# Decoder layer on one core: the feed-forward's preparation stands one batch later in the attention, Pool splits the router's weights, and the last two tiles' statistics go to the feed-forward

## What is computed

```python
x = x + retention(layernorm(x))                       # 8 heads, causal decay
x = x + cross_attention(layernorm(x), ctx, positions) # 32 heads of 16
h = layernorm(x)
router = h @ gate_w.T                                 # 8 experts, softmax, the two best
y = sum of the two chosen experts(h), each weighted by its probability
y = y + sigmoid(h @ shared_gate_w.T) * (silu(h @ s1.T) * (h @ s2.T)) @ sp.T   # 1408 wide
x = x + y
```

## Time and profile before

| | |
|---|---|
| median of 3 runs | 1491.64 us (1490.64 to 1492.25) |
| the profiled execution, its own time | 1494.26 us |
| its span in the profile | 1492.5 us |
| PE busy | 1339.0 us (90%) |
| DVE, ACT, POOL busy | 857.5, 485.4, 510.1 us |
| attention, rounds -1 to 9 | about 396 to 791 us of the span |
| round 7 | about 709 to 757 us |
| rounds 8 and 9 | about 757 to 791 us |
| feed-forward | 791.4 us to the end |

### The profile page before, as it was taken

The page is one execution under the profiler, slowest core; times in us unless marked ns, Lnnn a source line. Parts: engine busy times, 40 slices in busy tenths (PEclk is TensorE's granted clock), DMA queues, the critical chain, the costliest instruction groups (busy, mean ns, idle before and its releaser), DMA issues. The chain is left out here.

```text
span 1492.5 us, 24158 instructions
## 1 busy us (share of the span) xinstructions
PE 1339.0 (90%) x8442; PEld 1074.6 (72%) x8442; DVE 857.5 (57%) x1532; ACT 485.4 (33%) x755; POOL 510.1 (34%) x352
## 2 busy tenths in 40 slices
PE   5899999995499999999878999999999899999980
PEld 4677777773467766767547788888878799999970
DVE  5666666665487878778843556555575522222243
ACT  3222222223256555655645211111111123322320
POOL 1122221224444433335401007541160463575045
PEclk9999999998689999999989999999999999999995
DMA  8970000010565444555400003230000334343247
GB/s 320 324 237 1 0 0 0 0 53 4 182 175 169 139 146 146 157 155 158 122 2 22 1 22 143 90 138 22 22 22 29 134 132 142 134 145 135 82 134 246
DMA packets 84603, 159.83 MB, mean 107 GB/s; under 512 B 8528, under 2 KB 61904, under 8 KB 80976
## 3 DMA queue, kind: packets, MB, share of 16 engines
q1 hardware_dynamic: 78256, 124.19, 26.3%
q0 software_dynamic: 6272, 34.61, 6.6%
HBM read 109.22 MB, written 69.47 MB: 120 GB/s over the span
## 5 line engine op out<-in xcount | busy, mean ns | idle before, releaser
L1684 DVE SCALAR_TENSOR_TENSOR residual<-c_yp,c_shared,residual 128x512 f32<-128x512 f32 x176 | 127.2, 745 | 139.8 <-PE c_yp L43 135.5
L1051 DVE TENSOR_REDUCE b_mx<-b_rt 128x4 f32<-128x1024 f32 x128 | 156.3, 1221 | 54.2 <-PE b_rt L875 54.0
L1210 ACT ACTIVATE b_pf<-b_rt,b_zero 128x1024 f32<-128x1024 f32 x128 | 142.9, 1116 | 131.5 <-PE b_rt L887 131.2
L41 PE MATMUL c_fc<-c_xh,c_w 128*128 128x512 f32 x352 | 137.7, 391 | 0.0
L43 PE MATMUL c_fc<-c_xh,c_w 128*128 128x512 f32 x352 | 137.1, 389 | 0.0
L42 PE MATMUL c_fc<-c_xl,c_w 128*128 128x512 f32 x352 | 137.0, 389 | 0.0
L41 PE MATMUL c_fc<-c_ring,c_xTl 128*128 x312 | 105.2, 337 | 0.0
L1785 ACT ACTIVATE c_s<-c_fc 128x512 f32<-128x512 f32 x44 | 26.3, 598 | 229.3 <-PE c_fc L43 218.2
L43 PE MATMUL c_fc<-c_ring,c_xTh 128*128 x312 | 100.5, 322 | 0.0
L42 PE MATMUL c_fc<-c_ring,c_xTh 128*128 x312 | 100.2, 321 | 0.0
L1698 DVE TENSOR_TENSOR c_hTl<-c_eh,c_hTh 128x384 fp32r<-128x384 f32 x39 | 21.8, 558 | 136.5 <-ACT c_hTh L1809 136.5
(11 more groups left out here) (307 smaller groups left out, 3447.4 us busy)
## 6 DMA issues: line engine op xcount, KB each, us to landing
weights_b<-b_pack SPq DMA_DIRECT2D x128, 200.0 KB
c_eraw<-in_c_we POOLq DMA_DIRECT2D x8, 2176.0 KB, 9.8
b_pack<-b_hi SPq DMA_DIRECT2D x64, 256.0 KB, 2.5
c_rows_in<-in_b_ctx SPq DMA_DIRECT2D x39, 256.0 KB
c_rows_out<-in_b_ctx SPq DMA_DIRECT2D x39, 256.0 KB
c_xe<-c_rows_in SPq DMA_DIRECT2D x39, 256.0 KB, 2.9
c_rows_out<-c_ye SPq DMA_DIRECT2D x39, 256.0 KB, 2.0
c_wraw<-in_c_ws SPq DMA_DIRECT2D x11, 768.0 KB, 4.3
```

The source lines that it names most:

```text
L41: nc.tensor.matmul(out, ll, rh, start=start, stop=False)
L1051: nc.vector.tensor_reduce(out=mx[:, :, 2 * p:2 * p + 2].rearrange("p t e -> p e t"), in_=rt[:, 0:2, :].rearrange("p e (t s) -> p e t s", s ...
L1210: nc.scalar.activation(pf[:, s:s + 2, :], rt[:, 2:4, :], ACT.Exp, scale=XD ** -0.5, bias=zero[:, :]).then_inc(e_done, 1)
L1684: nc.vector.scalar_tensor_tensor(out=X[:, t, :], in0=yp[:, (n * 4 + k) % 3, :], scalar=shared[:, t:t + 1], in1=X[:, t, :], op0=ALU.mult, o ...
```

## The change

Of the lead-in, all but the loads and the last part moves from round 7 to round 8. In detail:

- `lead_shift` and `lead_low` (DVE), `lead_normal` and `lead_high` (ACT) and `lead_turn` (PE) stand in round 8; `lead_normal` at 1 to 4 where it stood at 2 to 5, the others at the same positions as before. `lead_loads` stays in round 7. `lead_turn` waits for one more batch's use of its two banks.
- ACT rounds the router's weights at position 0 of round 8. Pool does the subtraction for their low part, between its two weight splits, all three in one piece at position 0 of round 8, behind a wait for batch 7's last `negate`.
- The statistics of batch 7 (tiles 14, 15) are gone from round 9, and the root on Pool too. They stand at the head of the feed-forward's DVE list, behind `shift_by` of tiles 4 to 13; Pool's root comes after one more constant; `shift_by` of tiles 14, 15 stands behind the first `router_logits`, and ACT waits for it before the last two tiles.

```diff
@@ PE, cross attention
-                        pe.wait_ge(gm_read[BANK["w", n]], uses(B - 3, "w", n))
+                        pe.wait_ge(gm_read[BANK["w", n]], uses(B - 2, "w", n))
-                    if isinstance(b, int) and b == B - 1 and 4 <= i < 8:
+                    if isinstance(b, int) and b == B and 4 <= i < 8:
                         lead_turn(i - 4)
-                    if isinstance(b, int) and b == B - 1 and i == 10:
+                    if isinstance(b, int) and b == B and i == 10:
                         pe.wait_ge(lead.xl_done, 4)
@@ DVE, cross attention
-                    if isinstance(b, int) and b == B - 1:
+                    if isinstance(b, int) and b == B:
                         if i == 0:
                             lead_shift()
                         if 6 <= i < 10:
                             lead_low(i - 6)
-                        if i == 12:
-                            dve.wait_ge(lead.gwh_done, 1)
-                            nc.vector.tensor_tensor(lead.gwl[:, :, :], lead.graw[:, :, :], as_f32(lead.gwh[:, :, :]), ALU.subtract)\
-                                .then_inc(lead.gwl_done, 1)
-                    for d in due(i, live, 36):
-                        final_first(b + d, own)
-                    for d in due(i, live, 37):
-                        final_statistics(b + d, own)
+                    if not (isinstance(b, int) and b > B):
+                        for d in due(i, live, 36):
+                            final_first(b + d, own)
+                        for d in due(i, live, 37):
+                            final_statistics(b + d, own)
@@ ACT, cross attention
-                    if isinstance(b, int) and b == B - 1:
-                        if 2 <= i < 6:
-                            lead_normal(i - 2)
+                    if isinstance(b, int) and b == B:
+                        if 1 <= i < 5:
+                            lead_normal(i - 1)
                         if 5 <= i < 9:
                             lead_high(i - 5)
-                        if i == 11:
+                        if i == 0:
                             act.wait_ge(lead.const_in, 48)
                             nc.scalar.copy(lead.gwh[:, :, :], lead.graw[:, :, :]).then_inc(lead.gwh_done, 1)
@@ Pool, cross attention
-                    if isinstance(b, int) and b == B - 1 and i in (2, 10):
-                        lead_split(i // 10)
+                    if isinstance(b, int) and b == B and i == 0:
+                        pool.wait_ge(nm_done, 4 * B)
+                        lead_split(0)
+                        pool.wait_ge(lead.gwh_done, 1)
+                        nc.gpsimd.tensor_tensor(lead.gwl[:, :, :], lead.graw[:, :, :], as_f32(lead.gwh[:, :, :]), ALU.subtract)\
+                            .then_inc(lead.gwl_done, 1)
+                        lead_split(1)
-                    for d in due(i, live, 38):
-                        final_root(b + d)
+                    if not (isinstance(b, int) and b > B):
+                        for d in due(i, live, 38):
+                            final_root(b + d)
@@ Pool, feed-forward
+            nc.gpsimd.memset(power[:, :], -0.5).then_inc(presets, 1)
+            pool.wait_ge(presets, 4)
             pool.sem_inc(d_done, 1)
+            pool.wait_ge(var_done, 1)
+            nc.gpsimd.tensor_tensor(rstd[:, NT - TB:NT], var[:, NT - TB:NT], power[:, :].to_broadcast([P, TB]), ALU.pow).then_inc(rstd_done, 1)
             split(2)
@@ DVE, feed-forward
-            nc.vector.scalar_tensor_tensor(out=shift_by[:, 4:NT], in0=mean[:, 4:NT], scalar=-1.0, in1=rstd[:, 4:NT],
-                                           op0=ALU.mult, op1=ALU.mult).then_inc(shift_done, 1)
+            def shifts(a, b):
+                nc.vector.scalar_tensor_tensor(out=shift_by[:, a:b], in0=mean[:, a:b], scalar=-1.0, in1=rstd[:, a:b],
+                                               op0=ALU.mult, op1=ALU.mult).then_inc(shift_done, 1)
+
+            shifts(4, NT - TB)
+            for t in range(TB):
+                last = nc.vector.bn_stats(out=st[:, t, :], in_=X[:, NT - TB + t, :])
+            own.step(last)
+            for t in range(TB):
+                last = nc.vector.bn_aggr(out=mv[:, t, :], in_=st[:, t, :])
+            own.step(last)
+            own.step(nc.vector.tensor_copy(mean[:, NT - TB:NT], mv[:, :, 0]))
+            nc.vector.tensor_scalar(var[:, NT - TB:NT], mv[:, :, 1], EPS, None, ALU.add).then_inc(var_done, 1)
             low_x(4, 8)
@@ DVE, feed-forward, behind router_logits(n)
+                if n == 0:
+                    dve.wait_ge(rstd_done, 1)
+                    shifts(NT - TB, NT)
@@ ACT, feed-forward
             def normalize(a, b):
+                if b == NT:
+                    act.wait_ge(shift_done, 3)
```

## The result

| | before | after |
|---|---|---|
| median of 4 runs each | 1491.95 us | 1479.88 us (1477.01 to 1482.22) |
| ratio after to before | | 0.9917, 95% interval 0.9894 to 0.9939 |
| profiled execution, own time | 1494.26 us | 1482.22 us |
| its span | 1492.5 us | 1480.4 us |

Forecast were 1479.6 us and a span of 1480.5. In a second comparison on another occasion (`e8_after_again`, 6 runs beside 17 of before) the ratio was 0.9929, interval 0.9906 to 0.9952. So the change gains some 11 to 12 us. The total is as forecast; the rows behind it are not in every part, and that is what the rest is about.

The account below looks back on a forecast made before the run. PE was taken to bound the kernel, so gains before the feed-forward should arrive whole. Terms 7.3 - 0.7 + 3.0 + 2.4 = 12.0 us took the span from 1492.5 to 1480.5, giving 1479.6 us, range 1476 to 1486.

Parts of the forecast that it names:

- Round 7, (a), positions 5 to 11: Round 7, without the lead-in's transposes: position 12's rows start at 740.0, 2.6 us saved (1.0 to 3.6).
- (b), position 12: Round 7, position 12: taking the router's subtraction out of DVE's list saves 3.5 us (3.1 to 3.9).
- (c), the clock behind it: Round 7, behind PE's 4.93 us wait: products no longer run at the lower clock, 1.2 us saved (0 to 1.2).
- Round 7 in sum: Round 7, its three savings together: 7.3 us, from 4.1 to 8.7.
- Round 8: Round 8, with the lead-in's work added: net cost 0.7 us, between a gain of 1.0 and a cost of 5.6.
- the step on the clock: Round 8, values at position 9: added transposes bring PE to the upper clock level, some 0.9 us less.
- Round 9: Round 9 and the barrier: without the last statistics and Pool's root, PE starts at 788.6 instead of 791.59, 3.0 us saved.
- The clock at `router(0)`: Feed-forward's first products: upper clock from the start after the shorter gap, 2.4 us saved (0 to 2.7).
- The sum: Whole kernel: 7.3 - 0.7 + 3.0 + 2.4 = 12.0 us saved, span 1480.5.
- The signs of being wrong: 723.00 (PE's wait for maxima at round 7's position 4) moves; DVE stretched in round 8; feed-forward off 700.9 beyond 2.4.
- Pool would hold DVE in round 8: Rival, round 8: Pool's long instructions block DVE at the last scaling, up to 3.46 us, 1483.1; chance 0.05.
- The clock did not stay down: Rival: PE, thinly used, stays at the lower clock from 723 until the feed-forward, 16.3 us lost, 1495.9; chance 0.03.

Follow-up runs that it names:

- e8_after_again: The changed kernel itself, without a further edit, measured again on another occasion against the kernel before: ratio 0.9929.
- e9_split_late: The kernel before with only Pool's second weight split moved behind batch 7's last negation in round 8, DVE's subtraction left at position 12: ratio to before 0.9965.
- e2_stats_alone: The kernel before with only the last two tiles' statistics moved from round 9 to the feed-forward: ratio to before 0.9965.
- e3_gwl_alone: The kernel before with only the subtraction for the router's low part moved from DVE in round 7 to Pool in round 8: ratio to before 0.9963.
- e4_split_apart: The kernel before with only Pool's second weight split written at position 14 of round 7 instead of 10; Pool ran it as before: ratio to before 1.0003.
- e10_normal_early: The changed kernel with the shift and ACT's four normalizations back in round 7, transposes and splits still in round 8: ratio to before 0.9935.
- e7_splits_back: The changed kernel with Pool's two weight splits back in round 7, the router's subtraction still on Pool in round 8: ratio to before 0.9931.
- e6_fill: The changed kernel with the last statistics back in round 9, plus 14 useless PE products while they run: ratio to before 0.9931.
- e5_loads_at_2: The changed kernel with only the lead-in's five loads moved from position 1 to position 2 of round 7: ratio to before 0.9914.

## Why the prediction was right, point by point

- **Round 7, (a), positions 5 to 11.** The time of `rows` of position 12 was forecast as 740.0, that is 28.2 behind the first maximum (711.8); it is 744.00, 28.4 behind 715.60. That the total was met is luck, for the parts were not. Forecast were 1.0 up to `rows` of position 5 and 1.6 from there on. Measured are 2.4 up to there (727.03 is 11.43 behind the first maximum, where it was 13.83) and nothing from there on (16.97 to position 12, where it was 16.98). In `e8_after_again` it is 0.7 and 1.8. Over the kernels that mean the same as for the sum below, `rows` of position 12 comes 1.7 sooner. The transfer, too, did not land at a fixed time: it landed 3.0 later, while round 7 began 3.8 later. In the eleven executions with the loads ahead of it PE goes on 10.2 to 11.8 behind the round's first maximum, so it comes with the round.
- **(b), position 12.** Forecast 3.5 (3.1 to 3.9), measured 7.14 to 3.64: 3.5, but for the two executions with the lower clock at position 11 (5.09 and 5.41). The mechanism, DVE held by Pool's instruction, was argued from two rows and is shown by `e9_split_late`.
- **(c), the clock behind it.** Forecast 1.2; the changed kernel's last three positions took 7.42 and in its second execution 6.09, against 7.76, 7.87 and 7.79 of the old order: 0.3 to 1.8. Right in kind, not a number that one execution can give.
- **Round 7 in sum** was forecast as 7.3. Over three executions of the old order (43.56, 42.18, 41.89, mean 42.5) and four of the new one with its loads in place (37.31, 35.91, 38.14, 35.36, mean 36.7) it is 5.9. This term was mis-sized: the one profile of before is the slowest of its kind, by 1.0 above the mean, and (a) is 1.7 and (c) about 0.7 where 2.6 and 1.2 were forecast.
- **Round 8.** Forecast 1.6 late at position 8 and 0.9 back by the clock. Shown: 1.45 late, 22.70 against 21.25, in every kernel with the lead-in there, and nothing back: the slow values at position 9 were that execution's, since `e2_stats_alone`, `e3_gwl_alone`, `e4_split_apart` and `e9_split_late` run the old round 8 in 21.25. So the step on the clock failed. Of the 1.6, the 0.4 for normalizations is zero (`e10_normal_early`), and Pool's splits are nothing of it (`e7_splits_back`, 22.72). It lies with the transposes, ACT's copies and DVE's subtractions, which no run separates. That the stretch to X complete took its slow value in four of seven executions with the lead-in there and one of five without may be a further cost of up to a microsecond on the mean, or chance.
- **Round 9.** Forecast 3.0, measured 3.0; the statistics at the head of the feed-forward are covered, as the first `low_x` is at 788.76 and they end at 786.55.
- **The clock at `router(0)`.** Forecast 2.4, bound 2.7; measured 2.5 to 2.8, on the mean 2.7. `e6_fill` shows that it is PE's idleness: filling the gap is enough.
- **The sum.** By the table's means 5.9 - 1.45 + 3.0 + 2.7 = 10.2, and 11.2 with the 1.0 up to PE's last product that the prediction hadn't; by the runs 12.4 and 10.6. In the pair of profiles 12.1 = 6.2 in round 7, 1.5 to X complete, 3.0, 2.8 and 2.4 in the rest of the feed-forward, less the 3.8 with which round 7 began late. The span met to 0.1 us owes a good part to these cancelling. Of the last 2.4, 1.25 lie ahead of PE's last product, of which 1.0 is the term of the table that goes with the clock at `router(0)`; 1.1 lie in the end behind it, which no edit orders.
- **The signs of being wrong.** All three that the prediction named came: the transfer's 723.00 moved, DVE has a stretched instruction in round 8, and the feed-forward is 695.8 long, 5.2 less than 700.9 and not 2.4 (2.8 of it up to `up(0)`, 2.4 behind). The first two moved the sum little: the transfer came later by 3.0 with a round that began later by 3.8, and the stretched instruction cost nothing on the path. The third says that what is gained ahead of the feed-forward doesn't simply arrive whole at its end, as the prediction argued: its products took 1.0 less and its end varies by up to 4 us.
- **The rivals.** That Pool would hold DVE in round 8 came true beside the place named: not the last scaling but the copy ahead of it took 1.30 instead of 0.17, until Pool's instruction ended at 768.44. It took a third of the 3.46 and PE waited 0.45 for what stood behind it, which cost nothing by position 11, as `e7_splits_back` shows. The Trainium skill ("SBUF — State Buffer", Who interferes with whom) says that of the two the later one is blocked until the first has finished, and the row agrees: 767.16 + 1.30 is 768.46. The clock did not stay down: the granted clock is 0.82 in round 7 but 1.00 from 752.9 on.

## What to carry to other kernels

An instruction that is many times as long as its kind elsewhere in the trace may be waiting, not working: look for who runs beside it before moving it. In an in-order list a position times nothing unless something there waits, so to keep two engines apart takes a semaphore. And where the clock follows activity, one profile is one draw: read a term from the same stretch of several kernels before pricing it, and count a gap by the products behind it too.

## What the runs showed of the hardware that I had not expected

- A stretch with the same instructions took 8.54 or 10.15 us (to X complete), and round 7's position 4 to 5 took 3.37, 3.69, 4.53, 4.76 and 5.16 in five kernels that don't differ there.
- Whole runs of one kernel spread more than the sum's terms: 24 runs of before lay between 1484.73 and 1495.94.
- Fourteen products without a use, in a gap of 3.5 us that they don't lengthen, make the stage behind it 2.8 us shorter (6.44 to 3.64).
- The clock at `router(0)` goes with 1.0 us of the 650 that follow: 650.1 to 650.4 up to PE's last product in seven executions, 651.2 to 651.4 in the five others.
- Four small transfers that are issued at the same distance from the round's start land late or in time, depending on whether the loads stand ahead of them: PE waited 1.1 to 2.7 for them in eleven executions, and not at all in `e5_loads_at_2`.
